# A Toeplitz triangle of blocks in five products instead of six, with differences formed on VectorE

## The chip, the cores and the metric

The program runs on one core of one Trainium2 chip. The time is the device time of one execution in microseconds (us), the median of several runs. One core has a matrix engine (PE, TensorE), a vector engine (DVE, VectorE), a scalar engine (ACT, ScalarE), GpSimd (POOL), and a queue engine (SP) that issues transfers. The engines run side by side and wait for each other through semaphores. Only PE writes products, and only into PSUM, which has eight banks of 512 fp32 values on each of 128 partitions; ACT and DVE copy them out ("evict") to the main on-chip memory.

## What is computed

The reference is a small network of four parts on 4 images of 32 channels and 28x28 tokens: two convolutions with an L1-distance layer, a few feed-forward or attention steps chosen by the data, two quantised convolutions, and last a long causal convolution over the tokens. Only that last part changes. Cut to what matters:

```python
def _stu_conv(phi, u, n):        # phi: (L, K) filters, K = 16; u: (b, sl, d), sl = 784 tokens, d = 32
    Vf = jnp.fft.rfft(phi, n=n, axis=0)
    U_plus = jnp.fft.irfft(Vf[None, :, :, None] * jnp.fft.rfft(u, n=n, axis=1)[:, :, None, :], n=n, axis=1)[:, :sl]
    ...                          # U_minus: the same with every second token negated
out = jnp.einsum('btkd,k,kde->bte', U_plus, s, Mpp) + jnp.einsum('btkd,k,kde->bte', U_minus, s, Mpm)
...                              # four such sums over the first T, T/2, T/4, T/8 tokens, weighted and added
```

So each of 16 filters is convolved causally with each channel, and the results are mixed over filters and channels by small matrices.

## The kernel before

Everything runs in one program. The early stages are left as they are; the last one begins once the normalised tokens are ready.

**The last stage.** Even and odd tokens are treated apart, so a sequence has 392 places. A causal convolution is a product with a triangular matrix whose entry depends on the distance alone (Toeplitz). `HE` and `HO` (a part of `pool_`) hold, for each of the 16 filters, the strip of 392 (393) columns from which every 128-row block of that matrix can be cut: columns x to x+128 of the strip are the block x places from the diagonal. `UT` (a part of `WS2`) holds the tokens of both parities, turned so that places lie on partitions, in blocks of 128, 128, 128 and 8 places (i = 0 to 3), 32 channels for each of four images.

One unit of work u ("a filter" in what follows, 64 of them) is one image (b = u % 4), one group of four filters (g), one parity of the output (a2) and one parity of the strip (odd). `filtered(u)` multiplies token block i with the strip's first 392-128i columns and adds the result to PSUM bank u % 6 from column 128i on: products 392, 264, 136 and 8 columns wide. In units of 128x128 blocks that is a triangle of 3+2+1 blocks. Each product is four matmuls, one for each of the four filters kk of the group: weights of 32 columns, output on 32 partitions, so the four occupy different column groups of the array. In the trace each fp32 matmul appears as two MATMUL and two LDWEIGHTS entries.

ACT evicts even u and DVE odd u, 392 columns each, to slot u % 8 of `UEV`. After each four filters PE runs `mixed(grp-1)`, the mixing matrices on the group of four before (semaphores `uev_act`, `uev_dve`), into banks 6 and 7. `mixed` walks over `SEGS`, the ranges 0-49, 49-98, 98-196 and 196-392: products of 49, 49, 98 and 196 columns, 392 in all, of four matmuls each. Once, after group 12, `direct` adds a short lagged term from `ULAG`. At the end DVE adds the two halves to the tokens (L983) and SP stores them.

**Order.** PE's order is written out: 4 filters, mixed of the group before, and so on, `mixed(15)` last. A filter may reuse its bank when the eviction six filters earlier is done.

**Names that the steps touch.** `norm` (L577 on DVE) is the layer norm, used four times; its third use (k=2) stands ahead of the quantised convolutions. `turned` transposes tokens to PSUM banks 4 and 5; ACT (L536) and DVE (L972) copy these to `UT`. `UTD` and `HDE`/`HDO` are new names of the change. `arena` is scratch memory at the start of `pool_`. All matmuls show line L989, that of the helper `mm`.

Of the kernel before, what the change touches and what calls it, by code (L numbers as in the profile page):

```python
# [17 lines left out]
ALU = mybir.AluOpType  # L18
ACT = mybir.ActivationFunctionType
# [18 lines left out]
NK = 16  # L38
NPH = T // 2
# [57 lines left out]
def build(nc, x, par, con, ws1, wa1c, wa1r, ws2, wa2c, wa2r, amt, fmt, fwa, fwb, aw,  # L97
          cw1, cw2, phe, pho, mpp, mpm, mu, out):
    with ExitStack() as ctx:
# [6 lines left out]
        PS = ctx.enter_context(nc.psum_tensor("PS", [P, 8, 512], F32))  # L106


        X = sb("X", [P, T]); XN = sb("XN", [P, T])
        TMP = sb("TMP", [P, NIMG * PS_ * PS_])  # L110
        XC, SQ, SD, RS = (TMP[:, n * T:n * T + T] for n in range(4))
# [6 lines left out]
        arena = pool_[:, 0:2 * NQ * T]  # L118
        HO = pool_[:, 2 * NQ * T:].rearrange("p (k t) -> p k t", k=NK)
        HIDT = arena[:, 0:4 * T].rearrange("p (n t) -> p n t", n=8)  # L120
        UEV = arena[:, 0:4 * T].rearrange("p (n t) -> p n t", n=8)
        HE = sb("HE", [P, NK, NPH])
        QZ = sb("QZ", [P, 4, T])
        Y1R = QZ
# [19 lines left out]
        CEN = sb("CEN", [P, P])  # L144
        XS9 = Y1
        UT = WS2[:, 0:8, :]
        KEYS = Y1; QT_ = QZ[:, 0, :]
        NUM = RS; DEN = SD
        PT = arena[:, 0:PR * NIMG * QC[0]].rearrange("p (n b t) -> p n b t", n=PR, b=NIMG)
# [26 lines left out]
        def half(ap, h):  # L176
            return ap[:, h * HT:(h + 1) * HT]
# [12 lines left out]
        def bank(b, w=HT, rows_=slice(0, P)):  # L190
            return PS[rows_, b, 0:w]
# [17 lines left out]
        def by_image(src, n, c0=0, w=None):  # L209
# [9 lines left out]
            "ffn_wa ffn_wb att_w ffn_h1 hid_act hid_dve ffn_out ffn_h bias_kept att_proj keys_done q_done v_proj v_done "  # L219
            "sc_rise sc_done rise_out top_go st_done top_step top_split top_rows row_act row_dve exp_done acc_done den_done pv_done num_out den_out att_scaled att_wo att_h "  # L220
            "wmx_part wmx_rows wmx_row wmx_bc q_sc q_chain cq_chain cq_done x2_ready q_xin cc_done cv_relu cv_q x3_ready x3_sum "
            "wexp w_fill w_soft u_mixed w_chain sg_ready d_chain d_ready lags_in ut_done ut_act ut_dve u_plain u_done uev_act uev_dve mix_done y_ready stored"
        ).split()}
        ctx.enter_context(nc.allow_non_contiguous_dma("weights' rows are short"))
        block = ctx.enter_context(nc.Block())
# [125 lines left out]
        def _(a):  # L351
# [67 lines left out]
            for n in range(9 * CQ):  # L419
                g = CQ + n  # L420
# [4 lines left out]
                if n == 52:  # L425
                    a.wait_ge(s["u_mixed"], 4)
                    for lag in range(3):
                        q = slice(32 * lag, 32 * lag + 32)
                        a.activation(MUL[q, :, :], MUS[q, :, C * lag:C * lag + C], ACT.Copy).then_inc(s["d_ready"], 1)
                if n in (63, 66):  # L430
                    i = (n - 63) // 3
# [105 lines left out]
            a.wait_ge(s["zeroed"], 5)  # L537
            a.wait_ge(s["ln_out"], 8)
            a.activation(UPZ[:, 2:2 + T], URV[:, 1023:1023 - T:-1], ACT.Copy).then_inc(s["u_plain"], 1)
            for u in range(0, 64, 2):  # L540
                a.wait_ge(s["u_done"], u + 1)
                if u >= 8:
                    a.wait_ge(s["mix_done"], u // 4 - 1)
                a.activation(UEV[:, u % 8, :], bank(u % 6), ACT.Copy).then_inc(s["uev_act"], 1)  # L544


        @block.vector
        def _(v):
# [28 lines left out]
            def norm(k, src, dst, between=None, after=None):  # L577

                for h in range(2):
                    if k == 0:  # L580
                        v.wait_ge(s["ln_mean"], h + 1)
                        v.tensor_tensor(half(XC, h), half(src, h), bank(h), ALU.subtract).then_inc(s["ln_cent"], 1)
                    elif k == 2:
                        v.wait_ge(s["sx_sq"], v.snap(chosen, min_val=1, max_val=NB + 1) * 2 + (h - 1))
                        v.tensor_copy(half(XC, h), bank(4 + h)).then_inc(s["ln_cent"], 1)
                    else:
                        v.wait_ge(s["ln_sq"], 2 * (k - k // 3) + h + 1)
                        v.tensor_copy(half(XC, h), bank(h)).then_inc(s["ln_cent"], 1)
# [195 lines left out]
            for c in range(2):  # L784
                n = 4 - c
# [4 lines left out]
            for n in range(9 * CQ):  # L790
                g = CQ + n
# [147 lines left out]

            active_steps(v, code, step)  # L940

            norm(2, X, lambda h: half(XN, h))

            def hold(src, recip, low, high, tmp):

# [22 lines left out]

            v.wait_ge(s["zeroed"], 5)
            norm(3, X1, lambda h: URV[:, 1023 - h * HT:1023 - (h + 1) * HT:-1], None, summed)  # L970
            v.wait_ge(s["ut_done"], 2)
            v.tensor_copy(UT[:, 4:8, :], PS[:, 5, 0:512].rearrange("p (i m) -> p i m", i=4)).then_inc(s["ut_dve"], 1)  # L972
            for u in range(1, 64, 2):
                v.wait_ge(s["u_done"], u + 1)
                if u >= 8:
                    v.wait_ge(s["mix_done"], u // 4 - 1)
                v.tensor_copy(UEV[:, u % 8, :], bank(u % 6)).then_inc(s["uev_dve"], 1)  # L977
            v.wait_ge(s["x3_sum"], 1)
            x3 = X1[:, :].rearrange("p (t a) -> p t a", a=2)
            y = Y1[:, :].rearrange("p (t a) -> p t a", a=2)  # L980
# [6 lines left out]
        def _(t):  # L987
            def mm(out_, lhsT, rhs, start=True, stop=True):
                return t.matmul(out_, lhsT, rhs, start=start, stop=stop, skip_group_check=True)  # L989
# [67 lines left out]
            for h in range(2):  # L1057
                t.wait_ge(s["ln_out"], h + 1)
                for b in range(NIMG):
                    q = slice(32 * b, 32 * b + 32)  # L1060
                    last = mm(bank(4 - 4 * h + b), WS1[q, :], half(XN, h)[q, :])
# [54 lines left out]
            for n in range(9 * CQ):  # L1116
                if n == 8:
                    t.wait_ge(s["wmx_part"], 2)
                    for i in range(2):
                        last = mm(PS[0:1, 0, 128 * i:128 * i + 128], WMX[:, i:i + 1], con_("ident"))  # L1120
# [238 lines left out]
            def filtered(u):  # L1359

                grp, b = u // 4, u % 4
                g, a2, odd = grp // 4, (grp // 2) % 2, grp % 2
                c = a2 ^ odd
                if u == 4:
                    t.wait_ge(s["ut_dve"], 1)
                if u >= 6:
                    t.wait_ge(s["uev_act" if u % 2 == 0 else "uev_dve"], (u - 6) // 2 + 1)
                for i in range(4):
                    n = NPH - P * i
                    for kk in range(4):  # L1370
                        k = 4 * g + kk
                        if not odd:
                            m = HE[:, k, 0:n]
                        else:
                            m = HO[:, k, 1:1 + n] if a2 else HO[:, k, 0:n]
                        last = mm(PS[32 * kk:32 * kk + 32, u % 6, P * i:NPH], UT[:, 4 * c + i, 32 * b:32 * b + 32], m,
                                  i == 0, i == 3)
                last.then_inc(s["u_done"], 1)

            def mixed(grp):  # L1380

                g, a2, odd = grp // 4, (grp // 2) % 2, grp % 2
                t.wait_ge(s["uev_act"], 2 * grp + 2)
                t.wait_ge(s["uev_dve"], 2 * grp + 2)
                for lo, hi, sgm in SEGS:
                    for b in range(4):
                        last = mm(PS[32 * b:32 * b + 32, 6 + a2, lo:hi], ASEG[:, odd, sgm, 32 * g:32 * g + 32],
                                  UEV[:, (4 * grp + b) % 8, lo:hi], grp in (0, 2) and lo == 0, False)
                last.then_inc(s["mix_done"], 1)

            for grp in range(16):
# [120 lines left out]
```

## Time and profile before

| | |
|---|---|
| time, median of 3 runs | 366.26 us (362.93 to 367.12) |
| span of the profiled execution | 364.3 us |
| PE busy | 346.7 us, 95% of the span |
| PE weight loads busy | 212.4 us, 58% |
| DVE busy | 215.8 us, 59% |
| ACT busy | 178.7 us, 49% |
| last stage, from the first filter's matmuls to the wait ahead of `mixed(15)` | 258.47 to 359.86 us |

A row of the groups gives the engine, the operation, out<-in by the program's names, the shape, how often, then busy time and the mean duration of one in ns. Matmuls on different column groups overlap, so that the busy time of a group is much less than count times mean. A row of the timeline gives start, length, engine, line, operation and, in brackets, how long the engine had been idle and what released it; neighbouring instructions of one kind are merged (xcount).

### The profile page before, as it was taken

How to read it: one execution, taken by the hardware profiler on the slowest of the kernel's cores; microseconds unless marked ns; L12 is line 12 of the kernel's file. 1: busy time of each engine (PE TensorE's matmuls, PEld its weight loads, DVE VectorE, ACT ScalarE, POOL GpSimd, SP SyncE). 2: the span in 40 equal slices, each digit the busy share in tenths (PEclk: the TensorE clock that was granted, in tenths of full speed). 3: DMA queues.
4: the chain of work that ended last, by engine and by line, in shares of the span. 5: the costliest groups of instructions: out<-in, count | busy, mean ns of one | idle time of the engine just before them, and what ended most of it. 6: DMA issues, size and time to landing. Idle time of an engine off the chain costs nothing.

```text
span 364.3 us, 11456 instructions
## 1 busy us (share of the span) xinstructions
PE 346.7 (95%) x5077; PEld 212.4 (58%) x5077; DVE 215.8 (59%) x329; ACT 178.7 (49%) x180; POOL 21.2 (6%) x44
## 2 busy tenths in 40 slices
PE   8899999999999999899999998698999999999996
PEld 6437457743333345554663343465777778788884
DVE  2789999999999995455936785265211111111112
ACT  2862997887887952264828774312211111111110
POOL 4481000000000002000000000000000000000000
PEclk9999999999999999999989999999999999999999
DMA  5718300000000006400000000000230000000001
GB/s 171 222 21 266 122 2 2 2 3 2 2 2 0 2 2 234 137 7 12 1 2 2 3 1 2 7 0 2 67 71 2 4 4 4 4 4 2 4 4 46
DMA packets 10320, 13.12 MB, mean 36 GB/s; under 512 B 4106, under 2 KB 8988, under 8 KB 10264
## 3 DMA queue, kind: packets, MB, share of 16 engines
q1 hardware_dynamic: 9288, 9.11, 8.1%
q0 software_dynamic: 832, 3.00, 2.5%
q8 instruction: 43, 0.70, 0.8%
q10 hardware_dynamic: 144, 0.20, 0.2%
q14 instruction: 13, 0.11, 0.1%
HBM read 10.70 MB, written 0.40 MB: 30 GB/s over the span
## 4 chain that ended last, share of the span: by engine, by line
PE 57%; DVE 27%; SPq 7%; issue 4%; DMA 2%; ACT 2%; DVEq 0%; ACTq 0%
PE PS L989 57%; DVE pool_ L822 17%; SPq L238 3%; DMA W1R<-in_fwa 1%; DVE TMP L786 1%; DMA W4R<-in_aw 1%; SPq L232 1%; DVE pool_ L932 1%; DMA WA2R<-in_wa2r 1%; SPq L241 1%; SPq L243 1%; DVE pool_ L819 1%; SPq L245 1%; DVE MSC L735 0%; ACT pool_ L495 0%
## 5 line engine op out<-in xcount | busy, mean ns | idle before, releaser
L989 PE MATMUL PS<-pool_,CON 128*32 128x392 f32 (+2 forms) x1320 | 111.4, 493 | 0.7 <-ACT pool_ L495 0.2
L989 PEld LDWEIGHTS PS<-pool_,CON 128*32 128x32 f32 (+1 forms) x1320 | 49.0, 110 | 60.8 <-issue 43.7
L443 ACT ACTIVATE pool_<-TMP,WA 128x3136 f32<-128x3136 f32 x26 | 75.4, 2930 | 11.0 <-PE PS L989 10.8
L822 DVE TENSOR_SCALAR pool_<-TMP,WA 128x3136 f32<-128x3136 f32 x44 | 79.5, 1847 | 0.1
L977 DVE COPY pool_<-PS 128x392 f32<-128x392 f32 x32 | 18.1, 566 | 82.5 <-PE PS L989 82.5
L544 ACT ACTIVATE pool_<-PS 128x392 f32<-128x392 f32 x32 | 15.9, 498 | 83.3 <-PE PS L989 83.3
L989 PE MATMUL PS<-pool_,WS 128*32 128x392 f32 (+3 forms) x1024 | 46.6, 333 | 0.0
L989 PE MATMUL PS<-HE,WS 128*32 128x392 f32 (+3 forms) x1024 | 46.5, 333 | 0.1
L989 PEld LDWEIGHTS PS<-pool_,WS 128*32 128x32 f32 x1024 | 37.0, 110 | 10.0 <-issue 0.8
L989 PEld LDWEIGHTS PS<-HE,WS 128*32 128x32 f32 x1024 | 36.5, 111 | 10.7 <-issue 1.6
L989 PE MATMUL PS<-CON 128*128 128x196 f32 (+1 forms) x142 | 28.2, 337 | 1.1 <-DVE QZ L626 0.5
L989 PEld LDWEIGHTS PS<-CON 128*128 128x128 f32 x142 | 23.3, 192 | 9.0 <-issue 5.5
L495 ACT ACTIVATE pool_<-PS 112x896 f32<-112x896 f32 (+1 forms) x28 | 21.6, 822 | 6.8 <-PE PS L989 6.8
L903 DVE TENSOR_TENSOR pool_<-pool_ 112x1792 f32<-112x1792 f32 (+1 forms) x9 | 16.3, 1809 | 6.0 <-ACT pool_ L495 5.9
L989 PE MATMUL PS<-QZ,Y 32*112 32x448 f32 (+1 forms) x112 | 16.3, 567 | 0.1
L883 DVE CUSTOM_DVE_ANT_0 pool_<-PS,pool_ 112x392 f32<-112x392 f32 x28 | 13.8, 561 | 2.3 <-ACT pool_ L474 2.2
L989 PE MATMUL PS<-pool_,ASEG 128*32 128x49 f32 (+2 forms) x512 | 14.9, 248 | 0.1
L989 PE MATMUL PS<-Y,QZ 32*112 32x392 f32 x56 | 14.0, 529 | 0.0
L989 PE MATMUL PS<-pool_,QZ 32*112 32x392 f32 x56 | 12.4, 513 | 0.3 <-ACT pool_ L474 0.3
L474 ACT ACTIVATE pool_<-PS 112x784 f32<-112x784 f32 x14 | 11.3, 823 | 2.7 <-PE PS L989 1.7
L989 PE MATMUL PS<-pool_,VT 112*32 112x448 f32 (+1 forms) x112 | 12.1, 502 | 0.0
L989 PEld LDWEIGHTS PS<-QZ,Y 32*112 32x112 f32 x112 | 6.1, 182 | 9.5 <-issue 6.3
(237 smaller groups left out, 323.0 us busy)
## 6 DMA issues: line engine op xcount, KB each, us to landing
pool_<-in_pho SPq DMA_DIRECT2D x1, 3144.0 KB, 11.9
HE<-in_phe SPq DMA_DIRECT2D x1, 3136.0 KB, 11.8
QZ<-CW SPq DMA_DIRECT2D x12, 98.0 KB, 2.2
CW<-in_cw POOLq DMA_DIRECT2D x2, 576.0 KB, 4.8
CON<-in_con POOLq DMA_DIRECT2D x1, 732.5 KB, 5.6
out_y<-Y SPq DMA_DIRECT2D x1, 392.0 KB, 2.4
CQ<-in_ws SPq DMA_DIRECT2D x16, 9.0 KB
MPP<-in_mpp POOLq DMA_DIRECT2D x1, 256.0 KB, 3.1
```

What stands on the lines that cost most here:

```text
L232: sp.dma_start(PAR[q, 0:PC["cb"]], rows_).then_inc(s["par_in"], 16)
L238: sp.dma_start(WS2N[32 * b + 8 * g:32 * b + 8 * g + 8, :, :], bass.AP(ws2.tensor, (32 * g + 8 * b) * 9 * P + C * b, [[9 * P, 8], [P, 9], [ ...
L241: sp.dma_start(DMK[q, :], rows_).then_inc(s["sum_in"], 16)
L443: a.activation(unit, window(n // CQ), ACT.Abs, bias=WA2[:, n:n + 1], scale=-1.0).then_inc(s["act_unit"], 1)
L474: a.activation(RISE[0:QT, j % 2, 2 * p:2 * p + 2, :], PS[0:QT, 4 + 2 * p:6 + 2 * p, 0:HT], ACT.Relu).then_inc(s["rise_out"], 1)
L495: a.activation(PT[0:QT, st % PR, 2 * pair:2 * pair + 2, 0:QC[ch]], PS[0:QT, 2 * (u % 3):2 * (u % 3) + 2, 0:QC[ch]], ACT.Exp, scale=SCALE). ...
L544: a.activation(UEV[:, u % 8, :], bank(u % 6), ACT.Copy).then_inc(s["uev_act"], 1)
L822: v.tensor_scalar(unit, window(n // CQ), WA2[:, n:n + 1], None, ALU.max).then_inc(s["dve_unit"], 1)
L883: v.tensor_tensor_reduce(RISE[0:QT, j % 2, b, :], PS[0:QT, b, 0:HT], RISE[0:QT, j % 2, b, :], 1.0, -3.4e38, ALU.add, ALU.max, TOPS[0:QT, j ...
L903: v.tensor_tensor(ACC[0:QT, :, 0:w], PT[0:QT, (st - 1) % PR, :, 0:w] if i == 1 else ACC[0:QT, :, 0:w], PT[0:QT, st % PR, :, 0:w], ALU.add) ...
L977: v.tensor_copy(UEV[:, u % 8, :], bank(u % 6)).then_inc(s["uev_dve"], 1)
L989: return t.matmul(out_, lhsT, rhs, start=start, stop=stop, skip_group_check=True)
```

## The change

The triangle of a filter is computed in another way. Write S0, S1, S2 for the strip's columns from 0, 128 and 256, U0 to U3 for the token blocks. Before, output block 0 is S0U0, block 1 is S1U0+S0U1, block 2 (with its 8 columns of overhang) is S2U0+S1U1+S0U2 and the piece with U3. Now the kernel forms A=S1U1 (136 columns) and B=S0U0 (128) in a "low" bank, and in a "high" bank S2U0+S0U2 (136 columns twice, plus 8 with U3) and D=(S1-S0)(U0-U1) (128). Block 1 is D+A+B, block 2 is the high part + A. So the widths are 136, 128, 136, 136, 8 and 128.

ACT evicts the low bank (264 columns) of every filter; DVE, for every filter, adds three times: D+A, high+A, and (D+A)+B. A pair of banks is used for each filter, three pairs in turn. The differences U0-U1 (`UTD`, two of them) and S1-S0 (`HDE`, `HDO`, eight pieces of four filters) are formed by DVE: two strip pieces inside the third `norm`, six inside the loop over the filters, after u = 4, 8, 20, 24, 36 and 40. Each slot of `UEV` becomes 528 wide; `mixed` reads its last 392 columns.

```diff
@@ PE, filtered(u)
-                if u == 4:
+                if u == 2:
                     t.wait_ge(s["ut_dve"], 1)
-                if u >= 6:
-                    t.wait_ge(s["uev_act" if u % 2 == 0 else "uev_dve"], (u - 6) // 2 + 1)
-                for i in range(4):
-                    n = NPH - P * i
-                    for kk in range(4):
-                        k = 4 * g + kk
-                        if not odd:
-                            m = HE[:, k, 0:n]
-                        else:
-                            m = HO[:, k, 1:1 + n] if a2 else HO[:, k, 0:n]
-                        last = mm(PS[32 * kk:32 * kk + 32, u % 6, P * i:NPH], UT[:, 4 * c + i, 32 * b:32 * b + 32], m,
-                                  i == 0, i == 3)
-                last.then_inc(s["u_done"], 1)
+                if u >= 3:
+                    t.wait_ge(s["uev_act"], u - 2)
+                product(low, 0, QE, UT[:, 4 * c + 1, q], strips, QB, True)
+                product(low, QE, QB, UT[:, 4 * c, q], strips, 0, False).then_inc(s["u_low"], 1)
+                if u >= 3:
+                    t.wait_ge(s["uev_sum"], 2 * (u - 2))
+                product(high, QB, QE, UT[:, 4 * c, q], strips, 2 * QB, True)
+                product(high, QB, QE, UT[:, 4 * c + 2, q], strips, 0, False)
+                product(high, 2 * QB, QE - QB, UT[:, 4 * c + 3, q], strips, 0, False)
+                if b == 0 and a2 == 0:
+                    t.wait_ge(s["strip_diff"], 2 * g + odd + 1)
+                if u in (0, 4):
+                    t.wait_ge(s["ut_diff"], u // 4 + 1)
+                product(high, 0, QB, UTD[:, c, q], steps, 0, False).then_inc(s["u_done"], 1)
@@ ACT
-            for u in range(0, 64, 2):
-                a.wait_ge(s["u_done"], u + 1)
+            for u in range(64):
+                a.wait_ge(s["u_low"], u + 1)
                 if u >= 8:
                     a.wait_ge(s["mix_done"], u // 4 - 1)
-                a.activation(UEV[:, u % 8, :], bank(u % 6), ACT.Copy).then_inc(s["uev_act"], 1)
+                a.activation(UEV[:, u % 8, 0:QE + QB], bank(2 * (u % 3), QE + QB), ACT.Copy).then_inc(s["uev_act"], 1)
@@ DVE
-            norm(2, X, lambda h: half(XN, h))
+            norm(2, X, lambda h: half(XN, h), None, first_strips)
...
+            v.wait_ge(s["ut_act"], 1)
+            v.tensor_tensor(UTD[:, 0, :], UT[:, 0, :], UT[:, 1, :], ALU.subtract).then_inc(s["ut_diff"], 1)
             v.wait_ge(s["ut_done"], 2)
             v.tensor_copy(UT[:, 4:8, :], PS[:, 5, 0:512].rearrange("p (i m) -> p i m", i=4)).then_inc(s["ut_dve"], 1)
-            for u in range(1, 64, 2):
+            v.wait_ge(s["ut_dve"], 1)
+            v.tensor_tensor(UTD[:, 1, :], UT[:, 4, :], UT[:, 5, :], ALU.subtract).then_inc(s["ut_diff"], 1)
+            for u in range(64):
+                here, low = UEV[:, u % 8, :], bank(2 * (u % 3) + 1, QB + QE)
                 v.wait_ge(s["u_done"], u + 1)
-                if u >= 8:
-                    v.wait_ge(s["mix_done"], u // 4 - 1)
-                v.tensor_copy(UEV[:, u % 8, :], bank(u % 6)).then_inc(s["uev_dve"], 1)
+                v.wait_ge(s["uev_act"], u + 1)
+                v.tensor_tensor(here[:, QE + QB:QE + 2 * QB], low[:, 0:QB], here[:, 0:QB], ALU.add).then_inc(s["uev_sum"], 1)
+                v.tensor_tensor(here[:, QE + 2 * QB:UW], low[:, QB:QB + QE], here[:, 0:QE], ALU.add).then_inc(s["uev_sum"], 1)
+                v.wait_ge(s["uev_sum"], 2 * u + 1)
+                v.tensor_tensor(here[:, QE + QB:QE + 2 * QB], here[:, QE + QB:QE + 2 * QB], here[:, QE:QE + QB], ALU.add).then_inc(s["uev_dve"], 1)
+                if u % 16 in (4, 8) and u < 48:
+                    strip_step(u // 16 + 1, u % 16 // 8)
```

`product(to, at, w, lhs, strip, x0, start)` issues the four matmuls of one product, w columns wide, from column x0 of the strip to column `at` of bank `to`. QB is 128, QE is 136.

How this moves PE's instructions is best seen at the third group of four filters, whose strips are `HE` (a row is one or several matmuls in program order; `32x136` is the output's shape; `[waits ...]` names the semaphores). Before, the first two filters:

```order
L989 MATMUL PS<-HE,WS 32x392 [waits uev_act]
L989 MATMUL PS<-HE,WS 32x392 x3
L989 MATMUL PS<-HE,WS 32x264 x4
L989 MATMUL PS<-HE,WS 32x136 x4
L989 MATMUL PS<-HE,WS 32x8 x4
L989 MATMUL PS<-HE,WS 32x392 [waits uev_dve]
```

Now, the first filter and the start of the second (`TMP` is the memory in which `UTD` lies, `pool_` here that of `HDE`):

```order
L1018 MATMUL PS<-HE,WS 32x136 [waits uev_act]
L1018 MATMUL PS<-HE,WS 32x136 x3
L1018 MATMUL PS<-HE,WS 32x128 x4
L1018 MATMUL PS<-HE,WS 32x136 [waits uev_sum]
L1018 MATMUL PS<-HE,WS 32x136 x7
L1018 MATMUL PS<-HE,WS 32x8 x4
L1018 MATMUL PS<-pool_,TMP 32x128 x4
L1018 MATMUL PS<-HE,WS 32x136 [waits uev_act]
```

A filter has gone from 16 matmuls with one wait to 24 with two; none is wider than 136 columns.

On DVE, from the last `norm` to the end of the program, before:

```order
L598 TENSOR_TENSOR CW<-TMP,PS 128x392 [waits ln_bc] x2
L972 COPY WS<-PS 128x512 [waits ut_done]
L977 COPY pool_<-PS 128x392 [waits u_done] x4
L977 COPY pool_<-PS 128x392 [waits mix_done,u_done] x28
L983 TENSOR_TENSOR Y<-X,PS 128x392 [waits mix_done,x3_sum]
```

Now, from the same place to the first filter, and then at the first strip difference in the loop:

```order
L992 TENSOR_TENSOR TMP<-WS 128x128 [waits ut_act]
L994 COPY WS<-PS 128x512 [waits ut_done]
L996 TENSOR_TENSOR TMP<-WS 128x128 [waits ut_dve]
L1001 TENSOR_TENSOR pool_<-PS,pool_ 128x128 [waits uev_act,u_done]
L1002 TENSOR_TENSOR pool_<-PS,pool_ 128x136
L1004 TENSOR_TENSOR pool_<-pool_ 128x128 [waits uev_sum]
...
L953 TENSOR_TENSOR pool_<-HE 128x512
L1001 TENSOR_TENSOR pool_<-PS,pool_ 128x128 [waits uev_act,u_done]
```

One copy for every second filter has become three additions for every filter, and one subtraction now stands between ACT's copy of `UT` and DVE's.

In the third `norm`, two subtractions now stand between the reciprocal and the two products that wait for PE (`ln_bc`):

```order
L598 RECIPROCAL RSC<-SDC 128x98 [waits ln_sd]
L953 TENSOR_TENSOR pool_<-HE 128x512 [waits strip_in]
L951 TENSOR_TENSOR pool_<-pool_ 128x516
L603 TENSOR_TENSOR XN<-TMP,PS 128x392 [waits ln_bc] x2
```

Before, the reciprocal and the two products followed each other directly.

## Rows read from the trace of the kernel before

**Rows 1.** Page: busy tenths of each engine in 40 slices of the span
```profile
PE   8899999999999999899999998698999999999996
PEld 6437457743333345554663343465777778788884
DVE  2789999999999995455936785265211111111112
PEclk9999999999999999999989999999999999999999
```
**Rows 2.** Chain that ended last, 250 us to the end: start, length, what
```profile
258.47 101.39 PE PS L989 x2128
359.85 0.09 issue
359.95 0.92 PE PS L989 x29
```
**Rows 3.** Timeline 279 to 288: evictions of seven filters in a row, mixing between them
```profile
279.69 0.57 DVE L977 COPY pool_<-PS 128x392 f32<-128x392 f32 x1 [2.92 <-PE PS L989]
281.09 0.50 ACT L544 ACTIVATE pool_<-PS 128x392 f32<-128x392 f32 x1 [2.30 <-PE PS L989]
282.49 0.57 DVE L977 COPY pool_<-PS 128x392 f32<-128x392 f32 x1 [2.23 <-PE PS L989]
284.57 0.50 ACT L544 ACTIVATE pool_<-PS 128x392 f32<-128x392 f32 x1 [2.98 <-PE PS L989]
285.97 0.57 DVE L977 COPY pool_<-PS 128x392 f32<-128x392 f32 x1 [2.91 <-PE PS L989]
287.37 0.50 ACT L544 ACTIVATE pool_<-PS 128x392 f32<-128x392 f32 x1 [2.30 <-PE PS L989]
```
**Rows 4.** Timeline 250 to 263: the stage's start, weight loads, UT copies
```profile
257.73 0.60 ACT L536 ACTIVATE WS<-PS 128x512 f32<-128x512 f32 x1 [4.55 <-PE PS L989]
258.43 0.69 DVE L972 COPY WS<-PS 128x512 f32<-128x512 f32 x1 [1.77 <-PE PS L989]
258.47 5.02 PE L989 MATMUL PS<-HE,WS 128*32 128x392 f32 x101
258.80 0.15 PEld L989 LDWEIGHTS PS<-HE,WS 128*32 128x32 f32 x4 [0.18 <-issue]
259.13 0.90 PEld L989 LDWEIGHTS PS<-HE,WS 128*32 128x32 f32 x28 [0.17 <-issue]
260.13 0.50 ACT L544 ACTIVATE pool_<-PS 128x392 f32<-128x392 f32 x1 [1.06 <-PE PS L989]
```
**Rows 5.** Timeline 355 to 365: the last eviction and the last mixing
```profile
359.23 0.57 DVE L977 COPY pool_<-PS 128x392 f32<-128x392 f32 x1 [2.23 <-PE PS L989]
359.92 0.54 PEld L989 LDWEIGHTS PS<-pool_,ASEG 128*32 128x32 f32 x32 [0.45 <-issue]
```
**Rows 6.** Groups kept apart by shape: ACT and DVE operations nearest to the new ones
```profile
L544 ACT ACTIVATE pool_<-PS 128x392 f32<-128x392 f32 x32 | 15.9, 498 | 83.3 <-PE PS L989 83.3
L536 ACT ACTIVATE WS<-PS 128x512 f32<-128x512 f32 x1 | 0.6, 597 | 4.5 <-PE PS L989 4.5
L983 DVE TENSOR_TENSOR Y<-X,PS 128x392 f32<-128x392 f32 x2 | 1.1, 564 | 0.6 <-PE PS L989 0.6
L730 DVE TENSOR_TENSOR MSC<-MPP,MPM 128x512 f32<-128x512 f32 x2 | 1.4, 682 | 0.0
L735 DVE TENSOR_TENSOR MSC<-MSC,WSM 128x128 f32<-128x128 f32 x8 | 1.8, 280 | 0.0
L740 DVE SCALAR_TENSOR_TENSOR ASEG<-MSC,WSM,ASEG 128x128 f32<-128x128 f32 x6 | 2.1, 348 | 0.1
```
**Rows 7.** Timeline 226 to 243: DVE in the third norm and behind it
```profile
234.93 0.77 DVE L593 RECIPROCAL RSC<-SDC 128x98 f32<-128x98 f32 x1 [1.09 <-ACT SDC L360]
237.91 0.56 DVE L598 TENSOR_TENSOR XN<-TMP,PS 128x392 f32<-128x392 f32 x1 [2.22 <-PE PS L989]
240.03 0.36 DVE L947 TENSOR_SCALAR TMP<-TMP 128x392 f32<-128x392 f32 x1
240.43 0.37 DVE L953 TENSOR_SCALAR H1P<-TMP 128x392 bf16<-128x392 f32 x1
```
**Rows 8.** Transfers: queues over the span, then of 262 to 358 us
```profile
q8 instruction: 43, 0.70, 0.8%
...
q8 instruction: 20, 0.33, 1.3%
```

More of the change, by code:

```diff
@@ L44 @@
 LE, LO = NPH + 127, NPH + 128
+QB, QE = 128, 136
+UW = QE + NPH
 MAGIC = 12582912.0
@@ L120, in build @@
         HIDT = arena[:, 0:4 * T].rearrange("p (n t) -> p n t", n=8)
-        UEV = arena[:, 0:4 * T].rearrange("p (n t) -> p n t", n=8)
+        UEV = arena[:, 0:8 * UW].rearrange("p (n t) -> p n t", n=8)
+        HDE = arena[:, 8 * UW:8 * UW + NK * QB].rearrange("p (k t) -> p k t", k=NK)
+        HDO = arena[:, 8 * UW + NK * QB:8 * UW + NK * (2 * QB + 1)].rearrange("p (k t) -> p k t", k=NK)
         HE = sb("HE", [P, NK, NPH])
@@ L146, in build @@
         UT = WS2[:, 0:8, :]
+        UTD = SD[:, 0:2 * P].rearrange("p (c m) -> p c m", c=2)
         KEYS = Y1; QT_ = QZ[:, 0, :]
@@ L221, in build @@
             "wmx_part wmx_rows wmx_row wmx_bc q_sc q_chain cq_chain cq_done x2_ready q_xin cc_done cv_relu cv_q x3_ready x3_sum "
-            "wexp w_fill w_soft u_mixed w_chain sg_ready d_chain d_ready lags_in ut_done ut_act ut_dve u_plain u_done uev_act uev_dve mix_done y_ready stored"
+            "wexp w_fill w_soft u_mixed w_chain sg_ready d_chain d_ready lags_in ut_done ut_act ut_dve ut_diff strip_diff u_plain u_low u_done uev_act uev_sum uev_dve mix_done y_ready stored"
         ).split()}
@@ L940, in _, with strip_step, first_strips @@
             active_steps(v, code, step)
-            norm(2, X, lambda h: half(XN, h))
+            def strip_step(g, odd):
+                k = slice(4 * g, 4 * g + 4)
+                if odd:
+                    ins = v.tensor_tensor(HDO[:, k, :], HO[:, k, QB:2 * QB + 1], HO[:, k, 0:QB + 1], ALU.subtract)
+                else:
+                    ins = v.tensor_tensor(HDE[:, k, :], HE[:, k, QB:2 * QB], HE[:, k, 0:QB], ALU.subtract)
+                ins.then_inc(s["strip_diff"], 1)
+            def first_strips():
+                v.wait_ge(s["strip_in"], 32)
+                strip_step(0, 0)
+                strip_step(0, 1)
+            norm(2, X, lambda h: half(XN, h), None, first_strips)
             def hold(src, recip, low, high, tmp):
@@ L1378, in filtered, with product @@
-                last.then_inc(s["u_done"], 1)
+                q = slice(32 * b, 32 * b + 32)
+                low, high = 2 * (u % 3), 2 * (u % 3) + 1
+                strips, shift = (HO, a2) if odd else (HE, 0)
+                steps = HDO if odd else HDE
+                def product(to, at, w, lhs, strip, x0, start):
+                    for kk in range(4):
+                        last = mm(PS[32 * kk:32 * kk + 32, to, at:at + w], lhs, strip[:, 4 * g + kk, x0 + shift:x0 + shift + w], start, False)
+                    return last
@@ L1380, in mixed @@
+                product(high, 2 * QB, QE - QB, UT[:, 4 * c + 3, q], strips, 0, False)
[4 more added lines that the diff above has]
+                product(high, 0, QB, UTD[:, c, q], steps, 0, False).then_inc(s["u_done"], 1)
             def mixed(grp):
                 g, a2, odd = grp // 4, (grp // 2) % 2, grp % 2
-                t.wait_ge(s["uev_act"], 2 * grp + 2)
@@ L1384, in mixed @@
-                t.wait_ge(s["uev_dve"], 2 * grp + 2)
+                t.wait_ge(s["uev_dve"], 4 * grp + 4)
                 for lo, hi, sgm in SEGS:
@@ L1387, in mixed @@
                         last = mm(PS[32 * b:32 * b + 32, 6 + a2, lo:hi], ASEG[:, odd, sgm, 32 * g:32 * g + 32],
-                                  UEV[:, (4 * grp + b) % 8, lo:hi], grp in (0, 2) and lo == 0, False)
+                                  UEV[:, (4 * grp + b) % 8, QE + lo:QE + hi], grp in (0, 2) and lo == 0, False)
                 last.then_inc(s["mix_done"], 1)
```

## The prediction

> **What bounds the kernel now.** I read the page's slices first, then the chain of work that ended last, then the timeline of the last stage. In the slices PE is at nine tenths from the 29th slice to the last but one, where DVE stands at one or two tenths, and the granted clock is at its full level (2.4 GHz) there [rows 1]. The chain says it outright: from 258.47 us on it is 101.39 us of matmuls and nothing else, then 0.09 us of waiting, then the last mixing [rows 2]. Whatever PE saves in this stretch the kernel saves; a new wait of PE there costs its full length.
>
> The evictions show PE's pace, as each starts when its filter is done: 279.69, 281.09, 282.49, then 284.57, 285.97, 287.37 [rows 3]. So a filter takes **1.40 us**, and between 282.49 and 284.57 stands one mixing of 2.08-1.40 = **0.68 us**. Sixty-four filters are 89.6 us of the 101.39; the rest, mixings and the short direct part, is not touched.
>
> **PE, the main term.** What does a filter cost per column and what per product? The first product of a filter (392 columns, twice four entries) can be read from the weight loads: the matmuls start at 258.47, the loads of the second four at 258.80, and those of the next product at 259.13 [rows 4]. 0.66 us for 392 columns is 1.684 ns a column. The mixing puts 392 columns through in four products of 49 to 196 and takes 0.68 us [rows 3], hence 0.02 us more for three more products: some 0.005 us for each extra product, even when it is narrow. A filter has 392+264+136+8 = 800 columns: 1.347 us by that rate, and 1.40 is measured, so 0.053 us is left over. I put it on the 8-wide product, which is far too short to fill the time that its four loads need. That choice is mine, and the other end is below.
>
> Afterwards a filter has 136+128+136+136+8+128 = 672 columns: 1.132 us. The 8-wide product is still there (0.053), and two products more are 0.010. Sum **1.195 us**, 0.205 less; times 64, **13.1 us gained**. Bounds: if time went by columns alone, 0.16 of 1.40, i.e. 0.224 us a filter, 14.3 us. If the 0.053 lies on both narrow products of today (136 and 8) alike, 0.027 each, six narrow ones cost 0.16, a filter 1.29, and the gain is 7.0 us. The value taken lies near the first end, because the mixing's narrow products are cheap.
>
> A rule speaks against the change here. The Trainium skill ("TensorE: Matmul & The Clock Gate", Back-to-back issue gap) gives a stream of load and matmul pairs at 128 columns about 81 ns a matmul where its formula without loads gives 56, so narrow products would cost 1.45 times their columns. By that, as an estimate, the five products of 128 to 136 columns alone would take 664 x 1.684 x 1.45 = 1.62 us, a filter would be slower than today's 1.40, and the stage would lose 14 us or more. No such surcharge is in the mixing row above, whose products are narrower still.
>
> **PE's waits.** A filter now waits twice. The low bank waits for ACT's copy of the filter three before, the high bank for DVE's two reading additions of it. With a filter at 1.195 us, ACT and DVE get more than a filter's time to spare, as follows.
>
> **ACT.** 498 ns for 392 columns and 597 for 512 [rows 6] are 0.825 ns a column, so 264 columns cost 392 ns, once per 1.195 us. An eviction starts 0.26 us behind its filter's last column (258.47+1.40, then 260.13 [rows 4]), so this one starts 0.44+0.26 = 0.70 us into the filter and ends at 1.09, before the filter does; PE wants the bank at 3.59, 2.5 us later. Cost nothing. If that cover were gone, each wait would show at its length in PE's pace.
>
> **DVE.** 682 ns for 512 and 280 for 128 [rows 6] are 1.05 ns a column. An addition that reads PSUM took 564 ns at 392 [rows 6], so 288 ns at 128 and 296 at 136; the third, in main memory only, 280. Between dependent operations 0.04 us pass (0.36 us from 240.03, next at 240.43 [rows 7]). Together 0.86+0.12 = **0.98 us a filter**, from 0.57 every second filter. The strip pieces of 512 and 516 columns cost 0.68 us each; six stand in the loop. In sum 64 x 0.98 + 6 x 0.68 = 67 us, where PE takes 64 x 1.195 + 11.8 = 88 us. Even with every one of the three at 348 ns, the dearest 128-column row [rows 6], it is 64 x 1.16 + 4 = 78 us. The high bank of filter u-3 has been read 0.26+0.29+0.04+0.30 = 0.89 us after that filter ends, and PE wants it when it is 0.44 us into filter u, 2.83 us after that end: 1.9 us to spare. A strip piece takes 0.68 of them and is caught up at 0.2 us a filter. So DVE is hidden.
>
> **Start of the stage.** ACT's `UT` copy ends at 258.33 [rows 4]. DVE's subtraction then holds DVE to about 258.65, its own copy (0.69 us, formerly from 258.43) ends at 259.38 instead of 259.12, the second subtraction at 259.70. PE wants the first difference at the last product of filter 0, 258.47+0.98 = 259.45, the copied half at filter 2 (260.86), the second difference at filter 4. All in time.
>
> **The third norm.** The two subtractions, 1.37 us, fall into an idle time of 2.22 us of DVE, which waits for PE's products from 235.70 to 237.91 [rows 7]. Nothing. Without that gap they would cost 1.37 us.
>
> **The end.** Here DVE is exposed. Today the last copy starts at 359.23, takes 0.57, and PE begins the last mixing at 359.92 [rows 5]. Now three additions stand there, 0.94 us with their gaps: **+0.37 us**.
>
> **Sum.** -13.1+0.37 = -12.7 us. The profiled span of 364.3 becomes 351.6. The span lies within the runs (362.93 to 367.12), 2 us below their median; taking the same difference off the median, 366.26-12.7 = **353.5 us**.
>
> **Rivals.**
> *Narrow products cost more than I charge them* (chance 0.10): the bound above, 1.29 us a filter, 7 us gained, 359.5 us. For it speaks only that 0.053 us cannot be split by these rows; against it, the mixing.
>
> *Weight loads stop hiding, and it gets slower* (0.03). Four loads by themselves took 0.15 us (258.80 [rows 4]), while four matmuls of 136 columns last half of 136 x 1.684, 0.114 us. If each such set waited for its loads, ten sets at 0.15 and the 8-wide product at 0.067 make 1.57 us: +0.17 x 64 = 11 us, so 377 us. For it speaks that the weight-load row already stands at seven and eight tenths in this stage [rows 1]. It decides from 0.133 us a set upward. Against: 28 loads ran in 0.90 us (0.13 for four, and in no hurry) [rows 4], and 32 in 0.54 us in the last mixing [rows 5], 17 ns each, where the new filter needs 48 in 1.195, 25 ns each.
>
> *DVE becomes the bound* (0.02). It would need 1.3 us a filter; at 1.5 the stage would take 64 x 1.5+4 = 100 us, no change at 366. The dearest row gives 1.16.
>
> *The instruction supply becomes the bound* (0.03). The instruction queue moved 20 packets in 96 us, one in 4.8 us [rows 8]; PE's entries per group of four filters and a mixing rise from 320 to 448, in 5.5 us instead of 6.3, so one packet in 3.0 us. If 4.8 us were all it can do, a group would take 1.4 times 6.3 us, 8.8, and the kernel would be 40 us slower (406 us). But a packet keeps its one engine busy for only 0.008 x 16 x 364.3/43 = 1.1 us [rows 8], so I expect room. The Trainium skill ("Runtime: NRT & Kernel Launch", Instruction fetch mechanics) says the next block is fetched while the current one runs; no row here shows the fetch at the new rate.
>
> **How the numbers follow.** The main case (a gain of 11 to 14.5 us) gets 0.82, the rivals 0.10, 0.03, 0.02 and 0.03. The predicted time is the main case's. Low end: the columns-alone bound, 366.26-14.3 = 352, and 1.5 us for the spread of the runs about their median, 350.5. High end: 359.5, the first rival's time. About 1 in 10 is left outside. A change under 1% (3.7 us) can't be told from none in this kernel. Faster by over 1% is the main case and nearly all of the first rival, 0.91; within 1% gets 0.03 and slower 0.06.
>
> **What would show each step.** In the changed kernel's timeline: additions L1001 that start 1.2 us apart inside a group (1.29 for the first rival, 1.57 for the loads), and 1.9 us across a mixing; ACT's 264-column copy at 0.39 us; additions at 0.28 to 0.30 us; no idle time of PE ended by ACT or DVE in the stage but the last one, 0.8 us instead of 0.45; the third norm's L603 at its old distance from the reciprocal. Waits of PE for DVE every few filters, or weight loads with matmuls spaced beyond their columns, would prove me wrong.

## The result, and the profile after

The changed kernel takes **368.0 us** (median of 20 runs, 364.64 to 371.16) where the kernel before takes 364.93 us on the same chip (20 runs). The ratio is 1.0072, 95% interval 1.005 to 1.0094: slightly slower, not 12.7 us faster. Two of the 20 runs, 370.84 and 371.16 us, lie more than 1.5% above the fastest and are left out of the ratio. A second comparison (4 runs against 10) gave 369.34 against 364.62 us, ratio 1.0111 (1.0056 to 1.0166). The profiled execution spans 366.2 us, before 364.3.

The page of the changed kernel, slices of the span:

```profile
PE   8799999999999999889999998698989988899985
PEld 7437357743333336555653344565978978798874
DVE  1789999999999995446928765366554543444334
PEclk9999999999999999999999999789999999999999
```

Against [rows 1], DVE has gone from one or two tenths to three to five in the last stage, as it should, and the clock there is at its full level as before. But PE, formerly at nine tenths in the whole stage, now has slices of eight. The chain that ended last, of 264 to 290 us (start, length, what), shows where:

```profile
264.16 3.41 PE PS L1018 x106
267.57 0.69 issue
268.26 3.34 PE PS L1018 x95
271.60 0.66 issue
272.26 3.30 PE PS L1018 x97
275.56 0.15 issue
275.71 3.34 PE PS L1018 x95
279.06 0.11 issue
279.17 3.34 PE PS L1018 x95
282.50 0.39 issue
282.90 6.80 PE PS L1018 x203
```

[Rows 2] showed one unbroken piece of 101.39 us here. Now PE works for about 3.34 us and pauses for 0.1 to 0.7, again and again. "issue" means that PE waited for nothing the profile shows; no semaphore of ACT, DVE or a transfer of data ended the wait. The stretches between pauses have something in common. These are three of them, from one restart to the next (width; then the busy time and, in brackets, the count of PE matmuls, weight loads, DVE, ACT and POOL; last the granted clock, the share of DMA and GB/s):

```profile
268.25:272.25 4.00, 3.34 (x128) 3.07 (x128) 1.62 (x7) 0.78 (x2) 0.00 (x0) 1.00 0.39 91
272.25:275.70 3.45, 3.34 (x128) 3.21 (x128) 1.76 (x7) 1.17 (x3) 0.00 (x0) 1.00 0.02 5
293.50:297.20 3.70, 3.34 (x128) 3.07 (x128) 1.44 (x7) 0.78 (x2) 0.00 (x0) 1.00 0.02 4
```

Each holds 128 matmul and 128 load entries, **256 in all**, whatever filters and mixings happen to lie in it, and takes 3.45 to 4.0 us where PE shows 3.34 of work. By the matmuls' starts the stage has 27 full stretches of this kind, 3.69 us long on average. Together, of the stage's waits (who waited for whom: us in total, times, longest):

```profile
DVE pool_ L1001 <- PE PS L1018: 54.7, 61, 3.1
PEld PS L1018 <- issue: 14.9, 26, 1.0
PEld PS L1018 <- DVE pool_ L1004: 0.5, 1, 0.5
```

Weight loads sat idle for "issue" 26 times, 14.9 us in sum; for DVE only once, ahead of the last mixing. Before, the row for "issue" was much smaller:

```profile
PEld PS L989 <- issue: 2.9, 15, 0.4
```

Between pauses the filters run as forecast (timeline):

```profile
259.68 0.29 DVE L1001 TENSOR_TENSOR pool_<-PS,pool_ 128x128 f32<-128x128 f32 x1 [0.35 <-PE PS L1018]
260.87 0.30 DVE L1001 TENSOR_TENSOR pool_<-PS,pool_ 128x128 f32<-128x128 f32 x1 [0.50 <-PE PS L1018]
262.07 0.29 DVE L1001 TENSOR_TENSOR pool_<-PS,pool_ 128x128 f32<-128x128 f32 x1 [0.50 <-PE PS L1018]
263.26 0.29 DVE L1001 TENSOR_TENSOR pool_<-PS,pool_ 128x128 f32<-128x128 f32 x1 [0.50 <-PE PS L1018]
```

From 259.68 to 263.26 are three filters: 1.193 us each, and the 1.40 of [rows 3] has indeed gone. So 13 us were saved, and since the stage takes 102.9 us (258.22 to 361.13) where 88 were forecast, 15 us were lost. PE is shown idle for only 8.2 of these 15. The rest is hidden in the 3.34 us: from a restart the matmuls of a lot of 256 start within mostly 3.07 us, and then the last of them run out for some 0.27 us with nothing following them. That is lost too, as without a pause the next ones would start there. The work on 256 entries is therefore nearer to 3.1 us than to 3.34.

The instruction queue has a packet for every such stretch (262 to 358 us of the changed kernel: queue, packets, MB, share):

```profile
q8 instruction: 26, 0.43, 1.9%
```

26 packets in 96 us are one in 3.7 us, where [rows 8] had 20, one in 4.8. One packet of 0.43/26 MB = 16.5 KB per 256 entries: the theory is that PE's instructions arrive in packets of 256 entries, no faster than one packet in about 3.7 us.

### The profile page after: what moved, and what is told of

It reads as the page before. It is cut to its first block, busy times and chain, and to the rows that moved or that the text cites. A ratio compares the mean times of both kernels' runs of the same rounds, so it can differ in the third digit from the quotient of the medians.

```text
span 366.2 us, 13756 instructions
## 1 busy us (share of the span) xinstructions
PE 340.1 (93%) x6101; PEld 220.5 (60%) x6101; DVE 247.2 (68%) x499; ACT 187.9 (51%) x212; POOL 20.9 (6%) x44
## 4 chain that ended last, share of the span: by engine, by line
PE 56%; DVE 27%; SPq 7%; issue 6%; DMA 2%; ACT 2%; DVEq 0%; ACTq 0%
PE PS L1018 56%; DVE pool_ L827 17%; SPq L243 3%; DMA W1R<-in_fwa 1%; DVE TMP L791 1%; DMA W4R<-in_aw 1%; SPq L237 1%; DVE pool_ L937 1%; DMA WA2R<-in_wa2r 1%; SPq L246 1%; SPq L248 1%; DVE pool_ L824 1%; SPq L250 1%; DVE MSC L740 0%; ACT pool_ L500 0%
## 5 line engine op out<-in xcount | busy, mean ns | idle before, releaser
L549 ACT ACTIVATE pool_<-PS 128x264 f32<-128x264 f32 x64 | 25.1, 391 | 76.9 <-PE PS L1018 76.8
L1001 DVE TENSOR_TENSOR pool_<-PS,pool_ 128x128 f32<-128x128 f32 x64 | 18.6, 291 | 54.7 <-PE PS L1018 54.7
L1018 PE MATMUL PS<-pool_,WS 128*32 128x136 f32 (+2 forms) x1280 | 41.5, 257 | 2.8 <-issue 2.5
L1018 PE MATMUL PS<-HE,WS 128*32 128x136 f32 (+2 forms) x1280 | 40.7, 258 | 2.0 <-issue 1.9
L1018 PEld LDWEIGHTS PS<-pool_,WS 128*32 128x32 f32 x1280 | 39.4, 109 | 5.0 <-issue 4.9
L1018 PE MATMUL PS<-pool_,TMP 128*32 128x128 f32 x512 | 39.1, 275 | 2.0 <-issue 1.6
L1018 PEld LDWEIGHTS PS<-pool_,TMP 128*32 128x32 f32 x512 | 21.4, 112 | 3.2 <-issue 3.2
L1018 PE MATMUL PS<-pool_,ASEG 128*32 128x49 f32 (+2 forms) x512 | 18.3, 249 | 1.4 <-issue 1.2
L1002 DVE TENSOR_TENSOR pool_<-PS,pool_ 128x136 f32<-128x136 f32 x64 | 18.5, 289 | 0.0
L1004 DVE TENSOR_TENSOR pool_<-pool_ 128x128 f32<-128x128 f32 x64 | 18.0, 281 | 0.0
L1018 PE MATMUL PS<-QZ,Y 32*112 32x448 f32 (+1 forms) x112 | 15.2, 531 | 0.3 <-ACT pool_ L500 0.3
## 6 DMA issues: line engine op xcount, KB each, us to landing
HE<-in_phe SPq DMA_DIRECT2D x1, 3136.0 KB, 11.6
```

Source lines behind the costliest of these rows:

```text
L549: a.activation(UEV[:, u % 8, 0:QE + QB], bank(2 * (u % 3), QE + QB), ACT.Copy).then_inc(s["uev_act"], 1)
L1001: v.tensor_tensor(here[:, QE + QB:QE + 2 * QB], low[:, 0:QB], here[:, 0:QB], ALU.add).then_inc(s["uev_sum"], 1)
L1002: v.tensor_tensor(here[:, QE + 2 * QB:UW], low[:, QB:QB + QE], here[:, 0:QE], ALU.add).then_inc(s["uev_sum"], 1)
L1004: v.tensor_tensor(here[:, QE + QB:QE + 2 * QB], here[:, QE + QB:QE + 2 * QB], here[:, QE:QE + QB], ALU.add).then_inc(s["uev_dve"], 1)
```

## The experiments

Theory 1 is that supply. Theory 2: the pauses come from the second wait and the handshake with ACT and DVE that the change added. Theory 3: narrow products cost more than their columns. Entries in the stage are counted from the program: a filter of 4 products has 64, of 5 has 80, of 6 has 96; a mixing has 64, the direct part 128.

### Eight products, nothing else

The kernel before, its products cut up; columns, evictions and the one wait stay.

```diff
-                for i in range(4):
-                    n = NPH - P * i
+                for i, x, n in ((0, 0, 128), (0, 128, 128), (0, 256, 136), (1, 0, 128), (1, 128, 136), (2, 0, 68), (2, 68, 68), (3, 0, 8)):
                     for kk in range(4):
...
-                        last = mm(PS[32 * kk:32 * kk + 32, u % 6, P * i:NPH], UT[:, 4 * c + i, 32 * b:32 * b + 32], m,
-                                  i == 0, i == 3)
+                        last = mm(PS[32 * kk:32 * kk + 32, u % 6, P * i + x:P * i + x + n], UT[:, 4 * c + i, 32 * b:32 * b + 32],
+                                  strips[:, 4 * g + kk, x + shift:x + shift + n], i == 0 and x == 0, i == 3)
```

> The kernel before with the same 800 columns a filter, the same evictions and the same single wait, but cut into 8 products instead of 4 (128+128+136, 128+136, 68+68, 8), so that a filter is 128 instruction entries of PE instead of 64 and the stage 9344 instead of 5248. Theory 1, the supply of PE's instructions: in the changed kernel PE stops after every 256 entries, on average 3.64 us apart (103.6 us for 7296 entries). Then the stage needs 9344/256 x 3.64 = 133 us instead of 101.4, the kernel about 396 us, with 36 pauses each 256 entries apart. Theory 2, the pauses come from the new waits for ACT and DVE: there are none here, so only 4 x 0.005 us a filter are added, 1.3 us, 366 us. Theory 3, narrow products carry a fixed surcharge: the time rises evenly in every filter, without pauses; filters of the changed kernel ran at 1.20 us, which leaves room for 2 us at most.

Measured: **396.0 us** (2 runs), ratio 1.0829 (1.074 to 1.0919). Its chain, 300 to 316 us:

```profile
300.63 3.13 PE PS L989 x106
303.76 0.32 issue
304.09 2.99 PE PS L989 x99
307.07 1.39 issue
308.47 3.02 PE PS L989 x120
311.49 0.44 issue
```

The same pauses, 256 entries apart (35 stretches, 3.67 us on average), in a kernel without any of the change's waits, additions or differences. Theory 2 falls: it gave 366 us. Theory 3 falls too as the main cause, since the loss stands in pauses and not in the filters: filters without a pause follow each other at 1.42 to 1.45 us where they took 1.40, some 2 us in 64 filters of the 30 that the kernel lost.

### Six products, nothing else

The same edit with `((0, 0, 128), (0, 128, 264), (1, 0, 128), (1, 128, 136), (2, 0, 136), (3, 0, 8))`.

> The kernel before with 6 products a filter (128+264, 128+136, 136, 8), 96 entries as in the changed kernel, but 800 columns, its own evictions and one wait. Theory 1 (supply): 7296 entries need 28.5 x 3.64 = 103.7 us; PE's own work is 101.4+0.6 = 102.0 us. So 1 to 3 us over the kernel before, 366 to 368 us, with short pauses at some of the 256-entry boundaries: about the time of the changed kernel, though it computes 16% more columns. Theory 2 (waits): 0.6 us more, no pauses. Theory 3 (surcharge): 1 us more, no pauses.

Measured: 367.28 us (10 runs), ratio 1.0055 (1.0022 to 1.0087), 2.1 us more than before. Its chain of 264 to 290 us is one piece without an "issue":

```profile
264.00 26.08 PE PS L989 x765
```

With 800 columns a stretch of 256 entries takes PE 3.6 us by itself, just enough. The size, 2 us, was forecast by theory 1, but this run says little for it by itself: the chain of the whole stage holds no pause over 0.02 us, and theories 2 and 3 forecast 0.6 and 1 us more. The distances between evictions split the 2 us. Filters follow at 1.41 us instead of 1.40, 0.6 us in 64, which is what theory 2 gave for two more products. The other 1.3 us stand in a few longer distances, such as 2.30 us across a mixing where 2.08 to 2.09 are usual:

```profile
281.21 0.56 DVE L977 COPY pool_<-PS 128x392 f32<-128x392 f32 x1 [2.29 <-PE PS L989]
283.51 0.50 ACT L544 ACTIVATE pool_<-PS 128x392 f32<-128x392 f32 x1 [3.22 <-PE PS L989]
```

Each of the five longest of them holds the boundary between two lots of 256, and at one of these no entry starts for 0.33 us (from 307.09 on). So short pauses are there, mostly hidden under running matmuls; that all of the 1.3 us is due to them is not shown. What the run does show: with the entries of the changed kernel and 128 columns a filter more, it is as fast as the changed kernel (368.0).

### Without the 8-wide product

```diff
-                product(high, 2 * QB, QE - QB, UT[:, 4 * c + 3, q], strips, 0, False)
```

> The changed kernel without its 8-wide product (the last 8 places then lack their own block): 80 entries a filter, 6272 in the stage, all waits, evictions and additions as they are. Theory 1 (supply): 24.5 x 3.64 = 89 us of stage instead of 103.6, 14 us less, about 354 us, although the dropped product is only 0.06 us a filter (3.8 us) of work. Theory 2 (waits): the pauses stay, 4 us less, 364 us. Theory 3 (surcharge): 4 us less.

Measured: **350.92 us** (4 runs), ratio 0.9609 (0.9546 to 0.9673). Sixteen of 96 entries and 1% of the columns (8 of 672) are gone, and with them 17 us. The stage itself goes from 102.9 to 87.7 us, 15.2 less; the other 2 us lie ahead of it, where the code is the same (the stage begins at 255.54 us in this profile, in the others at 256.85 to 258.80). The product, sixteen entries in 0.06 us (filters now 1.13 us apart, before 1.19), is 3.8 us for 64 filters; the rest is pauses, whose sum in the waits falls from 14.9 to

```profile
PEld PS L1018 <- issue: 3.7, 10, 0.6
```

All the changed kernel's waits on ACT and DVE are still in this one.

### Every product cut to 8 columns

The disputed pace by itself: is it fixed, or a pause that follows each packet's work? This kernel leaves out most of what it should compute.

```diff
                 def product(to, at, w, lhs, strip, x0, start):
+                    w = min(w, 8)
```

> The changed kernel with every product of a filter cut to at most 8 columns (most of each output block is left out), all 24 matmuls, waits, evictions and additions as they are. PE's work on 256 entries falls from 3.34 us to about 1.9 (64 matmuls in sets of four at 0.028 us, mixings as before). Theory 1a, the instructions come at a fixed pace whatever PE does: while PE starves, 256 entries take 3.45 to 4.0 us as in the changed kernel and in the one with 8 products (means 3.69 and 3.67), so the stage stays at 28.5 x 3.5 to 3.7 = 100 to 105 us and the kernel at 364 to 369 us, though PE streams a tenth of the columns. Theory 1b, the next 256 entries are asked for only when PE has worked off the last, so a pause of 0.55 us is added to each: 28.5 x 2.45 = 70 us, which is also about what DVE's additions take (67 us), 332 us. Theories 2 and 3: no supply limit, DVE sets the pace, 67 to 72 us, 332 us.

Measured: **367.62 us** (5 runs), ratio 1.0061 (1.0017 to 1.0104), the changed kernel's time within 0.4 us, with hardly any columns left. Its chain, 311 to 328 us:

```profile
311.65 2.77 PE PS L1018 x120
314.42 1.23 issue
315.65 1.89 PE PS L1018 x96
317.54 2.11 issue
319.66 2.77 PE PS L1018 x120
322.43 0.95 issue
323.38 1.89 PE PS L1018 x128
325.28 1.84 issue
327.11 2.77 PE PS L1018 x99
```

The work between pauses shrinks to 1.9 to 2.8 us and the pauses grow to 0.95 to 2.1; from restart to restart it is 4.00, 4.01, 3.72 and 3.73 us, 3.77 on average over the stage. So the pace is fixed and independent of what the entries do (1a); a pause of constant length (1b) would have given 332 us. The granted clock was 0.53 in 262 to 346 us of this run, in which PE is busy for 55.6 of 84 us, so mostly the lower level of 1.2 GHz; the pace stayed the same, which fits. The run also rules out the weight loads as what sets the pace: from 315.65 on, 128 loads and 128 matmuls pass in 1.89 us, and then PE still stands until 319.66.

### The same algebra with 80 entries

If entries are the limit, the way out is fewer of them. Token block 0 is multiplied with two strip pieces, from columns 0 and 256; one matmul can take both.

```diff
-                product(low, 0, QE, UT[:, 4 * c + 1, q], strips, QB, True)
-                product(low, QE, QB, UT[:, 4 * c, q], strips, 0, False).then_inc(s["u_low"], 1)
...
-                product(high, QB, QE, UT[:, 4 * c, q], strips, 2 * QB, True)
-                product(high, QB, QE, UT[:, 4 * c + 2, q], strips, 0, False)
-                product(high, 2 * QB, QE - QB, UT[:, 4 * c + 3, q], strips, 0, False)
...
-                product(high, 0, QB, UTD[:, c, q], steps, 0, False).then_inc(s["u_done"], 1)
+                product(low, 0, QE, UT[:, 4 * c + 1, q], strips, QB, True)
...
+                product(low, QE, QB, UTD[:, c, q], steps, 0, False).then_inc(s["u_low"], 1)
...
+                for kk in range(4):
+                    row = strips[:, 4 * g + kk, shift:shift + NPH]
+                    both = bass.AP(row.tensor, row.offset, [row.ap[0], [2 * QB, 2], [1, QE]])
+                    mm(PS[32 * kk:32 * kk + 32, high, 0:2 * QE].rearrange("p (a t) -> p a t", a=2), UT[:, 4 * c, q], both, True, False)
+                product(high, QE, QE, UT[:, 4 * c + 2, q], strips, 0, False)
+                product(high, QE + QB, QE - QB, UT[:, 4 * c + 3, q], strips, 0, False).then_inc(s["u_done"], 1)
```

ACT copies A from the low bank and then B from the high one; DVE adds D+A, C+A (C is what the high bank holds beside B) and (D+A)+B. For a free bank PE now waits for `uev_sum` alone.

> The changed kernel in another arrangement, complete: the two products with token block 0 become one matmul of 272 columns (both strip pieces in one operand), the difference product goes to the first bank; 80 entries and 680 columns a filter, 5 products. ACT evicts twice a filter (136 and 128 columns), DVE adds as before. Theory 1 (supply): 6272 entries need 89 us; PE's work is 64 x 1.21 + 11.2 = 88.6 us, so the stage takes 89 to 91 us and the kernel 354 to 356 us, faster than both. Theory 2 (waits): as many waits as the changed kernel, the pauses stay, 367 us. Theory 3 (surcharge): two narrow products fewer, 1 us less than the changed kernel.

Measured: **353.55 us** (4 runs), ratio 0.9666 (0.9604 to 0.9729). The chain is whole again:

```profile
257.69 88.46 PE PS L1020 x2410
```

> The five-product arrangement once more, beside the changed kernel of the same call, to set the two against each other on one chip: 353 to 354 us against 367 to 368 us for the changed kernel.

> The changed kernel itself, for the comparison above: 367 to 369 us, 0.5 to 1% over the kernel before.

The repeat, side by side with the changed kernel: 354.95 us (4 runs; ratio 0.9715, 0.9672 to 0.9758) against the changed kernel's 369.34 (4 runs). In the profile of the repeat the weight loads have four short waits for "issue" again, 1.6 us in sum. The arrangement with 80 entries beats the changed kernel by 14.4 us and the kernel before by 9.7 to 11.6.

### All in one table

The same stretch, 262 to 346 us, of four kernels (before, changed, eight products, 80 entries), each row from its own trace:

```profile
262.00:346.00 84.00, 84.00 (x2156) 66.69 (x2152) 14.82 (x27) 13.44 (x27) 0.00 (x0) 1.00 0.06 14
```
```profile
262.00:346.00 84.00, 77.09 (x2928) 71.26 (x2922) 39.29 (x162) 20.01 (x52) 0.00 (x0) 1.00 0.06 15
```
```profile
262.00:346.00 84.00, 70.68 (x2912) 65.56 (x2906) 11.32 (x20) 10.45 (x21) 0.00 (x0) 1.00 0.06 15
```
```profile
262.00:346.00 84.00, 84.00 (x2950) 82.77 (x2942) 48.77 (x189) 34.06 (x121) 0.00 (x0) 1.00 0.06 14
```

Before, 4308 entries passed in 84 us, one lot of 256 in 5.0 us: far from the limit, PE busy throughout. In the changed kernel it is 5850 and in the one with eight products 5818, 3.68 and 3.70 us for 256, with PE busy for only 77 and 71 of 84 us. The last has 5892, 3.65 us, with PE busy all the time, and the kernel with six products has 5891: both sit just at the limit and are hardly held by it.

| kernel | products, columns a filter | entries of PE in the stage | these at 3.69 us for 256 | time, us |
|---|---|---|---|---|
| before | 4, 800 | 5248 | 76 | 364.6 to 365.2 |
| changed | 6, 672 | 7296 | 105 | 368.0; 369.3 |
| six products | 6, 800 | 7296 | 105 | 367.3 |
| all cut to 8 columns | 6, 48 | 7296 | 105 | 367.6 |
| eight products | 8, 800 | 9344 | 135 | 396.0 |
| without the 8-wide | 5, 664 | 6272 | 90 | 350.9 |
| 80 entries | 5, 680 | 6272 | 90 | 353.6; 355.0 |

Three kernels with the same entries and 800, 672 and 48 columns a filter take 367 to 369 us. Where the fourth column lies well below what PE's own work takes (before 101 us), the columns decide; where it lies well above, the entries do. Near the crossing it is only a rough guide, 2 to 3 us too high: for the stage six products took 103.4 us, 80 entries 88.5 and the kernel without the 8-wide product 87.7.

## Why the prediction was wrong

**PE's pace per column and product: right.** 1.195 us was forecast and 1.193 measured. The two terms that the rows left open are borne out as well: the 8-wide product is 0.06 us (1.19 with it, 1.13 without; 0.053 taken), and two more products add 0.01 us a filter (1.41 against 1.40; 0.010 taken). Neither the first rival (1.29) nor the one on weight loads shows up in any filter. That the kernel with 80 entries takes 353.55 us (354.95 in the repeat), near the forecast 353.5, is luck in its closeness: it has other products, 680 columns and another end.

**The rule of the Trainium skill** ("TensorE: Matmul & The Clock Gate", Back-to-back issue gap) that speaks for 81 ns a matmul at 128 columns is not borne out for matmuls that run four at a time on their column groups: the estimate from it was 1.62 us or more for a filter, and 1.193 us is measured.

**The signs I had named.** L1001 at 1.19 us inside a group and 1.87 across a mixing (where no pause lies between), ACT's copy at 0.39 us, additions at 0.28 to 0.30 and no wait of PE for ACT or DVE but the last: these came true, and the time was wrong all the same, as none of them looked at the supply.

The end of the stage in the changed kernel (timeline):

```profile
361.16 0.29 DVE L1001 TENSOR_TENSOR pool_<-PS,pool_ 128x128 f32<-128x128 f32 x1 [0.82 <-PE PS L1018]
361.37 0.29 DVE L1002 TENSOR_TENSOR pool_<-PS,pool_ 128x136 f32<-128x136 f32 x1
361.57 0.28 DVE L1004 TENSOR_TENSOR pool_<-pool_ 128x128 f32<-128x128 f32 x1
361.91 0.50 PEld L1018 LDWEIGHTS PS<-pool_,ASEG 128*32 128x32 f32 x32 [0.49 <-DVE pool_ L1004]
```

**ACT: right.** 391 ns for 264 columns (392 forecast). **DVE: hidden, as said,** but cheaper: the three additions start 0.21 us apart though each is 0.28 to 0.29 long, so a filter keeps DVE for some 0.7 us instead of 0.98.

**The start and the third norm: right.** No wait of PE for `UT` or the differences appears, and the first product behind the reciprocal starts 2.1 us after its end, as before (2.2 in [rows 7]):

```profile
233.57 0.77 DVE L598 RECIPROCAL RSC<-SDC 128x98 f32<-128x98 f32 x1 [1.15 <-ACT SDC L365]
236.45 0.56 DVE L603 TENSOR_TENSOR XN<-TMP,PS 128x392 f32<-128x392 f32 x1 [0.98 <-PE PS L1018]
```

**The end: over-charged.** From the last addition chain's start to the loads of the last mixing, 361.16 to 361.91, pass 0.75 us against 0.69 in [rows 5], not 0.37 more, again because the additions overlap.

**The instruction supply: the step that failed.** I had the mechanism as a rival, gave it 0.03, and computed what it needed, a packet in 3.0 us. (By its own numbers, 448 entries in 5.5 us, that is 3.1.) I then judged its room from how long a packet kept its transfer engine busy, 1.1 us, and so put the term at nothing. That is one part of the way of a packet, not its period; the row that spoke of the period (one in 4.8 us) came from a kernel that never had to wait for it, and so showed only that the queue can do at least that. The runs show the period: 3.67 to 3.77 us, of which the transfer is 1.1. With it the sum would have been 7296/256 x 3.69 = 105 us for the stage where I had 88, so +17-12.7, some 4 us slower; measured are 3.1 and 4.7. I had priced the rival at 40 us, with 4.8 us a packet, which also made it look far-fetched. The Trainium skill ("Runtime: NRT & Kernel Launch", Instruction fetch mechanics) says that the next block is fetched while the current one runs; the trace agrees, since each packet starts some 1.2 us after PE has begun a new lot and lands while PE works on it, and here that isn't enough, as a lot of 256 keeps PE busy for only 3.34 us.

**What the period is made of.** The packets' own start times and lengths in the traces show it. In the changed kernel, its repeat, the one with eight products and the one cut to 8 columns, every stretch between two restarts (111 in all) has exactly one packet. It starts 1.2 us after PE's restart on average (1.0 to 2.0), takes 1.1 us (0.9 to 1.6), and PE's next restart comes 1.4 us after its end (1.2 to 1.6): 3.7 us in sum. So these are three steps one behind another, and the queue moves data in less than a third of the period. By these figures it is the length of that round trip that limits PE here, not how much the queue can carry.

**What stays open.** Why a packet starts only when PE has begun a new lot, whether it holds the very next lot, as the distances suggest, and what fills the 1.2 us before and the 1.4 us behind it. While PE is starved, the period's values are mostly 3.45, 3.73 or 4.00 us, in steps of 0.27, for which no run has a reason. No run here changes anything on the fetching side.

## What to carry to other kernels

Count the matrix engine's instruction entries, not only its columns: here 256 entries took 3.67 to 3.77 us on average wherever PE was starved, and in no kernel less than about 3.6 over the stage. That is some 14 ns an entry, 58 ns for one fp32 matmul, which has four entries with its loads. A rewrite that cuts columns but adds matmuls pays in full only as long as each lot of 256 keeps the engine busy longer than that. When it doesn't, look for two products that share their weights and give them to one matmul with a two-part operand. And when a rival is a resource's rate, its price must come from a row in which that resource is the one waited for; a rate seen at ease says only that the resource can do at least that much, and the time that a transfer itself takes says nothing of the way around it.

## What the runs showed of the hardware that I had not expected

PE's entries pass at no more than 256 in 3.67 to 3.77 us on average in three starved kernels, with pauses 256 entries apart that the profile names "issue", and at about the same pace (3.77 against 3.69) at 0.53 of the full clock as at 1.00. Each lot has one packet of 16.5 KB; it starts some 1.2 us after PE has begun a lot, and PE goes on to the next one 1.4 us after it ends. Independent additions on DVE, one behind the other, start 0.21 us apart though each is shown as 0.29 us long.
